# A windowed-attention block on one core: 32-row score tiles in one run, four strips for values and sums, a written-out end

## The chip, the cores and the metric

One core of a Trainium2 chip runs the whole kernel. The metric is the device time of one execution in microseconds; the time before is the median of three executions. The trace and the page come from one further execution, taken with the profiler on.

## The reference

The input x has shape 4 x 96 x 128 x 128. All arithmetic is float32. Two layers are computed, cut here to what matters:

```
y  = layer_norm(x) over the 96 channels, rolled by (-4, -4), cut into windows of 8 x 8 = 64 tokens
q, k, v = y @ qkv_w.T + qkv_b          # 6 heads of 16 channels, q scaled by 1/4
p  = softmax(q @ k.T + mask)           # mask: -100 between parts of a window that wraps round the image
x  = x + (p @ v) @ proj_w.T + proj_b   # rolled back
x  = x + gelu(layer_norm(x) @ w1.T + b1) @ w2.T + b2     # 384 hidden channels
out = x * rsqrt(gamma @ (x * x) + beta)
```

The mask differs from zero in the last column of windows (side by side parts), in the last row of windows (upper and lower parts), and in the corner for both.

## The kernel before, in words

**Tiling.** A unit is one row of 16 windows (8 image rows, 1024 tokens). A half is 8 windows, 512 tokens. There are 64 units and 128 halves (`HALVES`). Within a half, two neighbouring windows form a pair (`PAIRS` = 4), since 2 x 64 tokens fill 128 partitions. Six heads form three head pairs.

**Rounds.** `rounds` (L221) walks over H; in every round each engine runs its list of stages once, each stage for another half: statistics and transposes of half H+4 (`TURN_IN`), normalised rows turned back of H+3 (`TURN_OUT`), q and k of H+1 (`QK`), scores, softmax and v of H (`ATTEND`), products with v of H-1, output projection of H-1 (`PROJECT`), first MLP product of H-2 (`MLP`), second of H-3 (`SETTLE`), the division at the end of H-4 (`DIVIDE`). The order in each list is written by hand in each engine's `steps` (PE L1035, ACT L602, DVE L819, POOL L489, SP L382), and semaphores hold the engines together. Rounds go on with has() guards until the last half has passed all stages.

**PE.** Precise products of 512 tokens go through `in_parts` (L897): three float32r products (high weight by high data, low by high, high by low). POOL's `split_hi`, `split_lo` (L430, L435) make the parts with two instructions over 512 columns each. Scores, v, products with v, and sums of probabilities are plain float32; each such matmul stands as two records in the profile.

**Scores** (`scores` L940). A half is done in two groups of two pairs. q and `k_block` lie in two row tiles of 64 partitions: three heads of 16 channels (48 rows), then eight mask rows, then zeros. `k_block` holds the keys in a block diagonal, so that one matmul of a 64 x 64 tile gives the scores of 3 heads, 64 tokens by 192 columns. A group is 8 matmuls into two PSUM banks. The mask costs no matmul of its own: SP brings mask rows into `y1_hi` each unit (`stage_mask` L322, `place_mask` L331), and the q product, with 105 rows and 128 output columns, passes them on. The two groups use the same two banks, so the second waits for `scores_shifted` of the first.

**Softmax.** For each group DVE takes the row maximum (`max_scores` L777) and subtracts it (`shift_scores` L782), both over 768 columns; ACT exponentiates (`softmax_exp` L556). PE turns the probabilities, three 128 x 128 transposes per pair, into `probs_t_bank` (`turn_probs` L962) and ACT copies 384 columns out (`probs_t_copy` L564), four times a half.

**Values and sums** (`times_v` L971, `sum_probs` L987). Each head pair m writes to its 32 columns of the array (PSUM partitions 32m to 32m+31): 24 matmuls of 64 columns, and three matmuls of 512 columns with a matrix of ones. 96 of the 128 array columns are used. ACT turns the sums into reciprocals with Ln and Exp; DVE multiplies (`divide` L792); POOL splits the product (`split_attended` L450).

**Banks.** Two PSUM banks, `mm_banks`, serve ten products a round in turn (`MM_ITEMS` L245). `mm_wait` (L866) makes a product wait until the one two places earlier has been read out. `turn_banks` serve the layer norms: one bank each takes the turned input and then the rows turned back.

**End of the kernel.** The last halves pass through the same rounds with ever fewer stages in them. A few stages of the last half go elsewhere (`split_last_hidden` L710, `split_last_squares` L722, and `mlp_up` into score banks).

## Time and profile before

| | us |
|---|---|
| median of 3 executions | 1937.88 (1937.69 to 1939.2) |
| the profiled execution's own time | 1939.82 |
| its span, first to last instruction | 1937.9 |
| PE busy | 1878.0 (97%) |
| PE weight loads busy | 1355.8 (70%) |
| DVE busy | 1610.0 (83%) |
| ACT busy | 1638.5 (85%) |
| POOL busy | 1645.4 (85%) |

The clock granted to TensorE is 0.993 of full speed on average. Busy time of an engine is the time in which at least one of its instructions has a record; records of consecutive instructions overlap a little, so the distance from one start to the next is the better price of an instruction in a row. PE's weight loads have rows of their own and run beside its matmuls. DMA engines are busy for 22% of the time.

### The profile page before, as it was taken

Reading aid. Unit: us, or ns where it says so; the run is one execution under the profiler, and the core shown is the slowest. Engines: PE = TensorE matmul, PEld = TensorE weight load, DVE = VectorE, ACT = ScalarE, POOL = GpSimd, SP = SyncE. Lnnn points to the kernel's source line nnn. Section 1 sums busy time; section 2 is a strip of 40 time slices with the busy share of each in tenths; the row PEclk is TensorE's granted clock in tenths of the full one; section 3 lists DMA queues with packets and bytes.
Section 4 is the critical chain, followed back from the end, with each engine's and each line's share of the span. In section 5 each row is a group of like instructions: output and inputs, shape, how many; then the busy total and the mean of one; then the engine's idle time right before and its main releaser. Section 6 shows DMA issues by size and latency. Waiting matters only on the chain.

```text
span 1937.9 us, 70164 instructions
## 1 busy us (share of the span) xinstructions
PE 1878.0 (97%) x26628; PEld 1355.8 (70%) x26628; DVE 1610.0 (83%) x4516; ACT 1638.5 (85%) x2945; POOL 1645.4 (85%) x1801
## 2 busy tenths in 40 slices
PE   5999999999999999999999999999999999999995
PEld 3677777777777777777777777777777777777773
DVE  5888888888888888888888888888888888888873
ACT  2788888888888888888888888888888888888884
POOL 4688888888888888888888888888888888888884
PEclk9999999999999999999999999999999999999997
DMA  3122222122122122122122122122122122122110
GB/s 62 28 42 50 35 51 50 35 51 50 35 51 50 34 52 50 33 53 50 32 54 50 32 53 50 32 53 49 34 53 44 38 52 49 35 51 50 26 31 25
DMA packets 217315, 85.00 MB, mean 44 GB/s; under 512 B 117287, under 2 KB 215913, under 8 KB 216985
## 3 DMA queue, kind: packets, MB, share of 16 engines
q1 hardware_dynamic: 216262, 80.22, 21.4%
q8 instruction: 216, 3.54, 0.8%
q14 instruction: 115, 0.93, 0.2%
q0 software_dynamic: 128, 0.20, 0.1%
q10 hardware_dynamic: 594, 0.12, 0.0%
HBM read 28.03 MB, written 25.17 MB: 27 GB/s over the span
## 4 chain that ended last, share of the span: by engine, by line
PE 95%; DVE 2%; issue 1%; DMA 1%; ACT 1%; SPq 1%; POOL 0%; POOLq 0%; DVEq 0%
PE mm_bank L900 49%; PE score_banks L956 11%; PE probs_t_bank L967 8%; PE pv_bank L981 6%; PE turn_bank L893 6%; PE mm_bank L991 6%; PE mm_bank L934 5%; PE turn_bank L886 4%; SPq L351 0%; DVE y_tok L750 0%; DMA k_block<-k 0%; DVE row_max L779 0%; DMA x_ext<-in_x 0%; DVE shifted L787 0%; DVE x L808 0%
## 5 line engine op out<-in xcount | busy, mean ns | idle before, releaser
L438 POOL TENSOR_TENSOR hidden_lo<-hidden,hidden_hi 128x512 fp32r<-128x512 f32 x382 | 484.6, 1282 | 0.2 <-POOL hidden_hi L433 0.2
L779 DVE TENSOR_REDUCE row_max<-score_banks 128x12 f32<-128x768 f32 x256 | 243.5, 951 | 152.7 <-PE score_banks L956 152.6
L520 ACT ACT_TABLE_LOAD x256 | 328.4, 1283 | 4.5
L750 DVE TENSOR_SCALAR y_tok<-turn_bank,moments,rstd 128x96 f32<-128x96 f32 x1024 | 304.8, 371 | 10.0 <-ACT rstd L531 5.6
L587 ACT ACTIVATE hidden<-mm_bank 128x512 f32<-128x512 f32 x381 | 228.0, 598 | 76.2 <-PE mm_bank L900 60.7
L560 ACT ACTIVATE probs<-shifted 128x768 f32<-128x768 f32 x256 | 216.2, 845 | 65.8 <-DVE shifted L787 65.5
L967 PEld LDWEIGHTS probs_t_bank<-ident_sb,probs 128*128 128x128 f32 x1536 | 200.0, 141 | 82.4 <-issue 2.4
L967 PE MATMUL probs_t_bank<-ident_sb,probs 128*128 128x128 f32 x1536 | 252.2, 272 | 1.4 <-ACT probs_t L566 1.4
L566 ACT ACTIVATE probs_t<-probs_t_bank 128x384 f32<-128x384 f32 x512 | 246.1, 481 | 7.6 <-PE probs_t_bank L967 7.6
L787 DVE TENSOR_TENSOR shifted<-score_banks,row_max 128x768 f32<-128x768 f32 x256 | 245.2, 958 | 8.8
L438 POOL TENSOR_TENSOR y_lo<-y,y_hi 96x512 fp32r<-96x512 f32 x128 | 218.8, 1709 | 23.8 <-POOL y_hi L433 23.3
L433 POOL TENSOR_SCALAR hidden_hi<-hidden 128x512 fp32r<-128x512 f32 x382 | 231.5, 617 | 2.1 <-ACT hidden L587 2.1
L956 PE MATMUL score_banks<-k_block,q 64*64 64x192 f32 x4096 | 227.0, 337 | 4.4 <-DMA k_block<-k 3.7
L956 PEld LDWEIGHTS score_banks<-k_block,q 64*64 64x64 f32 x4096 | 132.6, 133 | 137.6 <-issue 132.9
L739 DVE BATCH_NORM_STATS2 stats<-turn_bank 128x6 f32<-128x96 f32 x1024 | 190.2, 248 | 18.2 <-PE turn_bank L886 17.9
L433 POOL TENSOR_SCALAR attended_hi<-attended 96x512 fp32r<-96x512 f32 x128 | 79.2, 619 | 143.2 <-DVE attended L795 143.2
L438 POOL TENSOR_TENSOR attended_lo<-attended,attended_hi 96x512 fp32r<-96x512 f32 x128 | 165.4, 1293 | 23.8 <-POOL attended_hi L433 23.8
L438 POOL TENSOR_TENSOR x_sq_lo<-x_sq,x_sq_hi 96x512 fp32r<-96x512 f32 x127 | 162.1, 1276 | 23.6 <-POOL x_sq_hi L433 23.6
L900 PE MATMUL mm_bank<-y_hi,w_hi 97*128 97x512 f32 x381 | 171.9, 451 | 0.0
L900 PE MATMUL mm_bank<-hidden_hi,w_hi 128*96 128x512 f32 x384 | 163.0, 425 | 0.8 <-ACT log_den L592 0.7
L900 PE MATMUL mm_bank<-hidden_hi,w_lo 128*96 128x512 f32 x384 | 152.3, 397 | 0.0
L900 PE MATMUL mm_bank<-hidden_lo,w_hi 128*96 128x512 f32 x384 | 152.2, 396 | 0.0
(132 smaller groups left out, 4524.3 us busy)
## 6 DMA issues: line engine op xcount, KB each, us to landing
x_ext<-in_x SPq DMA_DIRECT2D x128, 192.0 KB, 3.3
k_block<-k SPq DMA_DIRECT2D x768, 32.0 KB, 2.1
out<-o_ext SPq DMA_DIRECT2D x128, 192.0 KB, 2.8
mask_stage<-in_qmask SPq DMA_DIRECT2D x64, 32.0 KB
y_hi<-mask_stage SPq DMA_DIRECT2D x64, 32.0 KB
k_block<-in_kmask POOLq DMA_DIRECT2D x2, 96.0 KB, 5.3
w_raw<-in_w_t SPq DMA_DIRECT2D x1, 144.0 KB
w<-in_w_t SPq DMA_DIRECT2D x1, 144.0 KB
```

The lines of the kernel that those rows point to most:

```text
L433: nc.gpsimd.tensor_scalar(hi, whole, 1.0, 1.0, ALU.mult, ALU.mult).then_inc(hi_ready, 1)
L438: nc.gpsimd.tensor_tensor(lo, whole, hi, ALU.subtract).then_inc(is_split, 1)
L520: nc.scalar.preload_act_table_set(name)
L560: nc.scalar.activation(probs[:, g, :, :, :, :].rearrange("t p j r k -> t (p j r k)"), shifted[:, g, :, :, :].rearrange("t i r k -> t (i r ...
L566: nc.scalar.activation(probs_t[:, a % 2, :, p, :], probs_t_bank[:, 0:HEAD_PAIRS * 128] .rearrange("k (p t) -> k p t", p=HEAD_PAIRS), ACT.C ...
L587: nc.scalar.activation(hidden[:, n, :], up_bank(A, a, n), ACT.Gelu).then_inc(gelu_ready, 1)
L750: made = nc.vector.tensor_scalar(y_tok[ln][:, c, :], turn_banks[ln][:, n * DIM:(n + 1) * DIM], moments[ln][:, c, 0:1], rstd[ln][:, c:c + 1 ...
L779: nc.vector.tensor_reduce(row_max[:, g, :, :], group_scores(), op=ALU.max, axis=AX.X)\
L787: nc.vector.tensor_tensor(shifted[:, g, :, :, :].rearrange("t i r k -> t r i k"), group_scores(), row_max[:, g, :, :].unsqueeze(3) .broadc ...
L900: made = nc.tensor.matmul(out, w, x_part, start=first and part == 0, stop=last and part == 2)
L956: made = nc.tensor.matmul(score_banks[64 * n:64 * n + 64, r, p * width:(p + 1) * width], q[rows, unit_slot(a), w * TOKENS:(w + 1) * TOKENS ...
L967: made = nc.tensor.transpose(probs_t_bank[:, m * 128:(m + 1) * 128], probs[:, g, at, m, :, :], ident_sb[:, :])
```

## The change

- Scores: `ROW_TILES` becomes 3. A row tile has 32 rows, which are exactly two heads (q and k in their natural order), so q, wq and y1_hi lose the mask rows and the padding; the q product has 97 rows and 96 output columns. `k_block` has 96 rows. All four pairs of a half are done in one run: 24 matmuls of 32 x 64 tiles and 128 columns, into three banks, one for each row tile (head pair).
- Mask: where a window has one, a further matmul adds it: four rows (`q_quadrants`) by 128 columns (`k_masks`), one for each row tile. That is the last window of each second half, and every window in the last row of windows. The mask DMAs of each unit go; nine small loads at the start take their place.
- Softmax in three groups of 512 columns (one bank each) in place of two of 768. The transposed probabilities go back into the score bank they came from, four transposes for each head pair, and ACT copies 512 columns, three times a half. `probs_t_bank` goes. The run of scores of a half therefore waits for the last copy of the half before (`probs_t_ready`).
- Values and sums on four strips: the fourth strip of 32 array columns takes the last pair of windows of all three head pairs. `times_v` still has 24 matmuls of 64 columns, `sum_probs` six matmuls (three of 384 and three of 128 columns). Ln and Exp of the sums run over 128 x 384. `divide` becomes four DVE instructions: three of 32 x 128 and one of 96 x 384.
- The rounding of the product with v moves from POOL to DVE (`round_attended`). POOL's other splits are taken apart so that an unrelated instruction stands between the two halves of a split.
- All lists and the order of the ten bank users are new. After the round of the last half a list written out by stage (`late`) takes the place of the remaining rounds, for every engine. In it the projection of the last half, the second MLP product and the denominators of the last two halves are plain float32 products without splits, and all Gelu evaluations of the last two halves stand behind one table load.

The core of the diff:

```diff
-ROW_TILES = 2
+ROW_TILES = 3
-GROUPS = 2
-GROUP_PAIRS = PAIRS // GROUPS
+GROUPS = HEAD_PAIRS
+STRIPS = HEAD_PAIRS + 1
+LAST = PAIRS - 1
+MAIN = LAST * 2 * TOKENS
...
         MM_ITEMS = [
-            ("v", ATTEND, v_ready, 1, 1), ("sum", ATTEND - 1, log_sum_made, 1, 1),
-            ("den", DIVIDE, log_den_made, 1, 1), ("k", QK, k_ready, 1, 1),
-            ("mlp2", SETTLE, x3_ready, 1, 1), ("q", QK, q_ready, 1, 1), ("proj", PROJECT, x2_ready, 1, 1),
-            *((f"mlp1_{n}", MLP, gelu_ready, HID_CHUNKS, n + 1) for n in range(HID_CHUNKS)),
+            ("sum", ATTEND - 1, log_sum_made, 1, 1),
+            ("k", QK, k_ready, 1, 1),
+            ("den", DIVIDE, log_den_made, 1, 1),
+            ("q", QK, q_ready, 1, 1),
+            ("mlp2", SETTLE, x3_ready, 1, 1),
+            ("v", ATTEND, v_ready, 1, 1),
+            ("proj", PROJECT, x2_ready, 1, 1),
+            ("mlp1_0", MLP, gelu_ready, HID_CHUNKS, 1),
+            ("mlp1_1", MLP, gelu_ready, HID_CHUNKS, 2),
+            ("mlp1_2", MLP, gelu_ready, HID_CHUNKS, 3),
...
+            def scores(A, a):
+                if has(A - 1):
+                    wait_alone(pe, probs_t_ready, GROUPS * A)
+                wait_alone(pe, q_ready, A + 1)
+                wait_alone(pe, keys_copied[a % 2], 16 * HEADS * (A // 2 + 1))
...
+                for p in range(PAIRS):
+                    cols, w = slice(p * width, (p + 1) * width), (a % 2) * HALF_WINDOWS + 2 * p
+                    for r, n in tiles:
+                        rows = slice(TILE_DIM * r, TILE_DIM * (r + 1))
+                        made = nc.tensor.matmul(score_banks[64 * n:64 * n + 64, r, cols],
+                                                q[rows, unit_slot(a), (w + n) * TOKENS:(w + n + 1) * TOKENS],
+                                                k_block[rows, w + n, :, :],
+                                                start=True, stop=mask_kind(A, w + n) is None)
+                    for r, n in tiles:
+                        kind = mask_kind(A, w + n)
+                        if kind is not None:
+                            rows = slice(TILE_DIM * r, TILE_DIM * r + QUADRANTS)
+                            made = nc.tensor.matmul(score_banks[64 * n:64 * n + 64, r, cols],
+                                                    q_quadrants[rows, :], k_masks[rows, kind, :, :],
+                                                    start=False, stop=True)
...
+                for turn in range(2 * LAST):
+                    at, n = turn // 2, turn % 2
+                    for strip in range(STRIPS):
+                        m, p = (strip, at) if strip < HEAD_PAIRS else (at, LAST)
+                        made = nc.tensor.matmul(pv_bank[32 * strip:32 * strip + 32, first:first + TOKENS],
+                                                v_block[:, (a % 2) * HALF_WINDOWS + 2 * p + n, m, :],
+                                                probs_t[:, a % 2, m, p, n * TOKENS:(n + 1) * TOKENS],
+                                                start=True, stop=True)
...
             def divide(A, a):
+                for m in range(HEAD_PAIRS):
+                    cols = slice(m * 2 * TOKENS, (m + 1) * 2 * TOKENS)
+                    nc.vector.tensor_tensor(attended[32 * m:32 * m + 32, MAIN:HALF], pv_bank[DIM:128, cols],
+                                            inv_sum[DIM:128, cols], ALU.mult)
+                nc.vector.tensor_tensor(attended[0:DIM, 0:MAIN], pv_bank[0:DIM, 0:MAIN],
+                                        inv_sum[0:DIM, :], ALU.mult).then_inc(attended_ready, 1)
+            def round_attended(A, a):
+                dve.wait_ge(attended_ready, A + 1)
+                nc.vector.tensor_copy(attended_hi[0:DIM, :], attended[0:DIM, :]).then_inc(attended_hi_ready, 1)
```

The new lists of a round (SP's is as before without the mask steps):

```
PE:   scores, sum_probs(H-1), times_v(H-1), k, denominators, turn_out(H-2), q, turn_probs 0, second MLP product,
      v, turn_out(H+3), turn_probs 1, project, turn_probs 2, turn_in(H+4), mlp_up 0, mlp_up 1, turn_in(H-1), mlp_up 2
DVE:  max 0, max 1, shift 0, normalise(H-2), shift 1, divide, max 2, round_attended, normalise(H+3), shift 2,
      second residual, split_y2, v_blocks, first residual, outputs, statistics(H+4), statistics(H-1)
ACT:  log table, rstd(H-2), rstd(H+3), log_sums, inverse_sums, k, exp 0, log_den, y(H-2), q, probs_t 0, inv_den,
      exp 1, exp 2, y(H+3), gelu table, probs_t 1, gelu 0, probs_t 2, gelu 1, gelu 2
POOL: split_hidden, wrap_out, rest_of_attended, wrap_x, square, round_y1, round_squares, rest_of_y1, rest_of_squares
```

## Rows read from the trace of the kernel before

**Rows 1.** The page, busy time: engine, busy us (share of span), instructions.

```profile
PE 1878.0 (97%) x26628; PEld 1355.8 (70%) x26628; DVE 1610.0 (83%) x4516; ACT 1638.5 (85%) x2945; POOL 1645.4 (85%) x1801
```

**Rows 2.** PE timeline, one round: start, us, engine, line, operation, out<-in, count.

```profile
961.56 0.88 PE L956 MATMUL score_banks<-k_block,q 64*64 64x192 f32 x16
962.37 0.89 PE L934 MATMUL mm_bank<-wv,y 97*32 97x48 f32 x64
963.08 1.09 PE L981 MATMUL pv_bank<-probs_t,v_block 128*32 128x64 f32 x48
963.97 1.06 PE L991 MATMUL mm_bank<-probs_t,ones_pair_sb 128*32 128x512 f32 x6
964.96 0.88 PE L956 MATMUL score_banks<-k_block,q 64*64 64x192 f32 x16
965.77 0.48 PE L900 MATMUL mm_bank<-x_sq_hi,wgdn_hi 97*96 97x512 f32 x1
...
967.25 0.49 PE L967 MATMUL probs_t_bank<-ident_sb,probs 128*128 128x128 f32 x3
967.57 1.04 PE L893 MATMUL turn_bank<-ident_sb,y_tok 128*96 128x128 f32 x8
...
971.33 0.40 PE L900 MATMUL mm_bank<-y_lo,wq_hi 105*128 105x512 f32 x1
971.75 0.44 PE L900 MATMUL mm_bank<-attended_hi,wproj_hi 97*96 97x512 f32 x1
...
973.10 0.48 PE L900 MATMUL mm_bank<-y_hi,w_hi 97*128 97x512 f32 x1
...
975.65 0.49 PE L967 MATMUL probs_t_bank<-ident_sb,probs 128*128 128x128 f32 x3
976.07 0.88 PE L956 MATMUL score_banks<-k_block,q 64*64 64x192 f32 x16
```

**Rows 3.** DVE timeline of the same round, with idle time before and its releaser.

```profile
962.51 0.96 DVE L779 TENSOR_REDUCE row_max<-score_banks 128x12 f32<-128x768 f32 x1 [1.19 <-PE score_banks L956]
963.50 0.96 DVE L787 TENSOR_TENSOR shifted<-score_banks,row_max 128x768 f32<-128x768 f32 x1
964.38 1.11 DVE L768 COPY v_block<-mm_bank 64x384 f32<-64x384 f32 x2
965.52 2.38 DVE L750 TENSOR_SCALAR y_tok<-turn_bank,moments,rstd 128x96 f32<-128x96 f32 x8
967.81 0.68 DVE L795 TENSOR_TENSOR attended<-pv_bank,inv_sum 96x512 f32<-96x512 f32 x1
968.41 0.94 DVE L779 TENSOR_REDUCE row_max<-score_banks 128x12 f32<-128x768 f32 x1
...
972.69 0.69 DVE L800 TENSOR_TENSOR x<-mm_bank,x_ext 96x512 f32<-96x512 f32 x1 [0.49 <-PE mm_bank L900]
973.36 0.76 DVE L739 BATCH_NORM_STATS2 stats<-turn_bank 128x6 f32<-128x96 f32 x4
```

**Rows 4.** Waits, 200 to 1800 us: us in total, times, longest.

```profile
DVE row_max L779 <- PE score_banks L956: 130.6, 110, 1.2
```

**Rows 5.** Instructions of POOL L438, L433 and DVE L716: duration min/median/max in ns.

```profile
L438 POOL TENSOR_TENSOR y_lo<-y,y_hi x128: 1248/1786/1819, 15.5 to 1846.1; 96x512 fp32r<-96x512 f32 x128
L433 POOL TENSOR_SCALAR x_sq_hi<-x_sq x127: 616/618/2103, 83.7 to 1918.1; 96x512 fp32r<-96x512 f32 x127
L716 DVE CAST hidden_hi<-hidden x2: 413/836/1258, 1917.0 to 1918.1; 128x512 fp32r<-128x512 f32 x2
```

**Rows 6.** The chain that ended last, its end: start, us, what.

```profile
1877.48 0.85 PE score_banks L956 x16
...
1915.70 0.76 DVE x L808
...
1928.21 0.76 DVE x L808
...
1929.71 0.43 DVE x_sq_hi L730
```

More of the change, by code:

```diff
@@ L51 @@
 X_SLOTS = 4
-QKV_CONSTS = 8
-MLP_CONSTS = 14
+QKV_CONSTS = 6
+MLP_CONSTS = 9
 MLP_WEIGHTS = 4
@@ L227, in rounds, with late @@
                 steps(run, H)
+        def late(stage, A, *rest):
+            stage(A, A % (2 * X_SLOTS), *rest)
         def has(at, count=HALVES):
@@ new lines, in window_block, with mm_bank @@
+        MM_ORDER = [(item[0], H + item[1]) for H in range(-TURN_IN - 1, HALVES) for item in MM_ITEMS
+                    if has(H + item[1])] + MM_FINISH
+        MM_PLACE = {item: place for place, item in enumerate(MM_ORDER)}
+        MM_EMPTIED = {item[0]: item[2:] for item in MM_ITEMS}
+        def mm_bank(name, A):
+            return mm_banks[MM_PLACE[name, A] % len(mm_banks)]
+        def mm_bank_emptied(name, A):
+            place = MM_PLACE[name, A] - len(mm_banks)
+            if place < 0:
+                return None
+            other, B = MM_ORDER[place]
+            semaphore, per_half, own = MM_EMPTIED[other]
+            return semaphore, per_half * B + own
@@ L502, in _ @@
             rounds(steps)
+            late(split_hidden, FINAL - 2)
+            late(wrap_out, FINAL - 4)
+            late(square, FINAL - 2)
+            late(round_squares, FINAL - 2)
+            late(rest_of_squares, FINAL - 2)
+            late(wrap_out, FINAL - 2)
+            late(wrap_out, FINAL)
         @block.scalar
@@ L847, in _ @@
             rounds(steps)
+            late(normalise, FINAL - 1, 1)
+            late(divide, FINAL)
+            late(split_y2, FINAL - 1)
+            late(first_residual, FINAL)
+            late(second_residual, FINAL - 2)
+            late(statistics, FINAL, 1)
+            late(outputs, FINAL - 3)
+            late(normalise, FINAL, 1)
+            late(split_y2, FINAL)
+            late(second_residual, FINAL - 1)
+            late(last_squares, FINAL - 1)
+            late(outputs, FINAL - 2)
+            late(second_residual, FINAL)
+            late(last_squares, FINAL)
+            late(outputs, FINAL - 1)
+            late(outputs, FINAL)
         @block.tensor
@@ L1062, in steps @@
                     w1_bias_product()
-                last = H == HALVES - 1 - MLP
-                if not last:
-                    run(mlp_up, MLP, 0)
+                run(mlp_up, MLP, 0)
+                run(mlp_up, MLP, 1)
                 run(turn_in, PROJECT, 1)
-                if not last:
-                    run(mlp_up, MLP, 1)
-                    run(mlp_up, MLP, 2)
-                run(turn_probs, ATTEND, 3)
+                run(mlp_up, MLP, 2)
             rounds(steps)
+            late(times_v, FINAL)
+            late(sum_probs, FINAL)
+            late(turn_out, FINAL - 1, 1)
+            late(denominators, FINAL - 3)
+            last_project()
+            for n in range(HID_CHUNKS):
+                late(mlp_down, FINAL - 2, n)
+            late(mlp_up, FINAL - 1, 0)
+            late(turn_in, FINAL, 1)
+            late(mlp_up, FINAL - 1, 1)
+            late(turn_out, FINAL, 1)
+            late(mlp_up, FINAL - 1, 2)
+            late(denominators, FINAL - 2)
+            for n in range(HID_CHUNKS):
+                late(mlp_up, FINAL, n)
+            last_mlp_down(FINAL - 1)
+            last_mlp_down(FINAL)
+            last_denominators(FINAL - 1)
+            last_denominators(FINAL)
 def kernel(x, L0_conv_norm1_w, L0_conv_norm1_b, L0_conv_qkv_w, L0_conv_qkv_b, L0_conv_proj_w,
```

455 lines of the change are left out of this document (212 added, 243 removed).

## The prediction

> **What bounds the kernel now.** I read the page first [rows 1]: PE is busy for 97% of the span, the other engines for 83 to 85%. A sum over stages would already point to PE, but the share of busy time of pipelined matmuls proves little, so I went to the timeline of one round [rows 2]. There the reader should lay start against start: every PE group begins when the one before it has drained; the only stall inside the round is 0.18 us between the end of the q product (971.33 + 0.24) and the projection (971.75). A round, from one first run of scores to the next, takes 976.07 - 961.56 = 14.51 us. Then the DVE timeline [rows 3]: its list is one dense run with two holes, 1.19 us before the first maximum and 0.49 us before the first residual, both ended by PE. The wait list says that this is so in all rounds [rows 4]: 110 waits in 1600 us, 130.6 us in all. So PE's own work sets the round, DVE has 1.68 us of room, and its occupied time is 14.51 - 1.68 = 12.83 us. The end of the kernel is different [rows 6]: 60.4 us lie between the last half's first scores (1877.48) and the end of the span, and there single engines wait for each other.
>
> **PE's work after, without waits.** What a tiled plain product costs can be read from four groups [rows 2]. Each moves 3072 columns (records x columns). Spread over four tiles, 768 each, they take 0.71 (v, 962.37 to 963.08) and 0.81 us (scores). Over three strips, 1024 each, they take 0.89 (values) and 0.99 (sums). So 256 columns more in every tile cost 0.18 us, and I use that as the price.
> - Scores: 48 records x 128 = 6144 columns in six tiles, 1024 each: 0.81 + 0.18 = 0.99 us, once, in place of twice 0.81. No row has six tiles at once; the bounds are 0.99 and, if only four run at a time, 1536 columns a tile, 1.35 us. I take 0.99, since 2 x 2 tiles already run side by side at the rate of four strips.
> - Values: 0.89 - 0.18 = 0.71. Sums: 0.99 - 0.18 = 0.81. The bounds are these and no gain (0.89, 0.99).
> - Masks: in every second half three matmuls, 256 columns a tile, 0.18 us; in the last of 16 rows of windows 24 matmuls over six tiles, about 0.72 us. On average 0.5 x 15/16 x 0.18 + 0.72/16 = 0.13 us a round.
> - Transposes of probabilities: twelve as before, in three groups for four. v, k, q, denominators, projection and MLP: same columns, so the same slots. Fewer rows and output columns of q change nothing: column count sets these slots.
> - Wait and row moves: DMA of masks goes from SP's queue; it was off the path, worth 0.
>
> Before its first turn_out, PE now does scores 0.99, sums 0.81, values 0.71, k and denominators 1.48 (965.77 to 967.25): 3.99 us. From turn_out to the next scores it took 976.07 - 967.57 = 8.50 us; take off the 0.18 stall, add v 0.71 and three transposes 0.32 (967.25 to 967.57, the fourth group that used to stand earlier): 9.35 us. PE alone: 3.99 + 9.35 + 0.13 = 13.47 us a round, 1.04 less than now.
>
> The Trainium skill ("TensorEngine Tiling (Array Packing)", Tiling Modes) says that 32 x 64 gives eight independent tiles and that changing the mode drains the engine; by its first part the six tiles cost the 0.99 above, and no run here shows it yet.
>
> **DVE's work after** [rows 3]. A subtraction takes 0.88 us start to start for 768 columns (963.50 to 964.38) and the product `attended` 0.60 for 512 (967.81 to 968.41): 0.28 per 256 columns. So each of three maxima and three subtractions costs 0.60, 3.60 in all, against two pairs of 0.99 + 0.88, 3.74: -0.14. `divide`: the large piece 0.60 - 0.14 = 0.46; three pieces of 128 columns between a statistics instruction of 96 columns (0.76 us for four, 0.17 each) and a normalisation of 96 columns (965.52 to 967.81 for eight, 0.29). I take 0.20, near the first, because it has no scalars from memory either: 1.06 in all, +0.46; bounds 0.97 and 1.42. The rounding: 0.43 us in [rows 6], 0.35 start to start. DVE then holds 12.83 - 0.14 + 0.46 + 0.35 = 13.50 us, almost exactly what PE holds. Its 1.68 us of room are gone, and so latency around the round decides.
>
> **What is late next.** I count from the start of a run of scores, masks left out. DVE's first maximum starts 0.95 us after a run of 0.81 (962.51 - 961.56), so at 1.13 after one of 0.99.
> - Loop 1. max, max, shift to 2.93; four normalisations (2.29/2) to 4.08, the last one's tail and signal to 4.23. PE arrives at turn_out of H-2 at 3.99 and waits 0.24. Behind this wait stand q, all later products and the next scores: 4.23 + 9.35 + 0.13 = 13.71 us. It also means that what the values and sums save is mostly waited away: without their 0.36 PE would arrive at 4.35.
> - Loop 2. DVE goes on: shift 0.60, divide 1.06, max 0.60, rounding 0.35, normalise 1.15, shift 0.60, second residual 0.66 (its slot before the 0.49 hole, duration less overlap), split_y2 0.60, v_blocks 1.14 (964.38 to 965.52). The end is at 10.84; with the signal, mlp_up 0, which uses v's bank, may start at 10.94. From there to the next scores PE needs 976.07 - 973.10 less a transposes group, 2.65: 13.59 + 0.13 = 13.72. PE itself would come at 10.93. The two loops tie.
> - The rounding on DVE against POOL [rows 5]. Here two casts in SBUF took 413 and 1258 ns, the second beside a POOL instruction; POOL's rounding took 616 ns as a rule and 2103 once, at that same moment. y_lo took 1248 ns at the start and 1786 in the rounds. Now the rounding stands where POOL is just finishing the split of the hidden values, every round. Bounds: 0 and 0.84 us on loop 2. I take 0.23, since POOL's split should end at about that time.
>
> The Trainium skill ("SBUF — State Buffer", Who interferes with whom) has this as an exclusive lock held for a whole instruction; the trace agrees, with 1258 against 413 ns. By that rule alone the cost would be nothing or the rest of a POOL instruction, never a share.
>
> Other new waits have cover: the next scores wait for the last copy of transposed probabilities, which ACT can do at about 13.0, 0.7 before; the key copies start 2 us earlier in the round than now; POOL gets its last part of the product at 6.8 and has until 9.6. ACT's groups change by -0.2 us. If these covers were gone each would cost its overlap, 0.1 to 0.7.
>
> A round: 13.72 + 0.23 = 13.95 us, 0.56 less. Some 124 of the 128 rounds are full: 69.4 us.
>
> **The end** [rows 6]. Between the second residuals of the last two halves lie 12.5 us, in which POOL splits squares for one and DVE hidden values for the other. In the new list three plain products lie there; one moves 1024 columns, at most 0.99 us, say 2.6 for three: 9.9 us less. The cast of the last square and its rest, about 1.1, go. With the other splits I take 13; bounds 5 and 20. The start I leave at 0.
>
> Sum: 69.4 + 13 = 82.4. Against the profiled execution: span 1937.9 to 1855.5, its own time 1939.82 to 1857.4. The median shown is 1.94 below the latter, so the forecast is 1855.5.
>
> **Rivals.**
> - PE bound (0.15). The normalisation and v_blocks are never late; for it: 0.24 us is a small miss and orders can absorb it. Then 13.47 a round, 129 + 13 = 142: 1796. Against: both loops miss it by the same amount.
> - Six tiles do not run together (0.18). For it: no row shows more than four. Scores 1.35, and since both loops begin with them the round is 14.31: 25 + 13 = 38, 1900.
> - DVE lock, on the other side (0.20). The rounding is blocked each round for the 0.84 of [rows 5], 0.61 more than I took, and the divide pieces cost 0.32 each, 0.36 more; v_blocks comes 0.97 later, mlp_up 0 waits, and the round is 14.92. That is +51 - 13 = +38: 1976. It decides from 0.66 us above what I took (0.56, plus 13/124); the lock alone gives 14.56, 1931. Against: DVE could only be blocked so long if POOL started a long instruction just before, every time.
> - The forecast, two tied loops at 13.75 to 14.15 (0.47): 1830 to 1880.
>
> A difference of 0.2%, 3.9 us, is about what a measurement of this kernel can tell. Faster: 0.47 + 0.15 + 0.15 + 0.04 = 0.81; slower 0.15; same 0.04. The range 1795 to 1935 holds all but half of the lock's case and the outer part of the PE case.
>
> **What would show it.** Scores in 0.99 us and values in 0.71: the price by tile is right. A wait of turn_out for the normalisation of about 0.2 us, or of mlp_up 0 for v_blocks, in each round: the loops. The rounding at 0.42 with few at 1.2: the lock is small. DVE idle before its first maximum below 0.5 us. I am wrong if scores take over 1.3 us, if PE waits for something on ACT or POOL, or if PE has no wait at all.

## The result, and the profile after

| | before | changed |
|---|---|---|
| median | 1938.54 us (1937.69 to 1940.3, 4 runs) | 1890.55 us (1888.51 to 1891.02, 4 runs) |
| profiled execution's own time | 1939.82 | 1888.51 |
| its span | 1937.9 | 1886.6 |
| round, start of scores to next, median | 14.51 | 14.07 (first halves of a unit), 14.25 (second halves) |
| last scores to the end of the span | 60.4 | 55.4 |

The changed kernel takes 0.9749 of the time before (95% interval 0.9732 to 0.9766), 48 us less. The forecast was 1855.5: the direction is right, the size was to be 82 us. The time lies inside the wide range on record (1795 to 1935) but outside the band of the forecast's own case (1830 to 1880), and nearer to the rival in which six tiles don't run together (1900) than to the forecast. All the accounting below is between the two profiled spans: 51.3 us less, where 82.4 were forecast, so 31.1 us are to be explained.

The page, busy time by engine, the row that answers to [rows 1]:

```profile
PE 1829.9 (97%) x30179; PEld 1376.4 (73%) x30179; DVE 1729.0 (92%) x5278; ACT 1586.8 (84%) x2950; POOL 1538.1 (82%) x1661
```

DVE went from 83% to 92%. PE still shows 97%, as before, and this says little: the holes that matter in a round are of 0.05 to 0.2 us and lie inside the modelled tails of its records. They are read from starts. This is the PE timeline of one round of a first half (no masks) in the middle of the kernel, to be laid beside [rows 2]; columns are start, us, engine, line, operation, out<-in, count.

```profile
936.81 1.12 PE L996 MATMUL score_banks<-k_block,q 32*64 32x128 f32 x48
937.86 0.52 PE L1037 MATMUL mm_bank<-probs_t,ones_pair_sb 128*32 128x384 f32 x3
...
938.53 0.86 PE L1027 MATMUL pv_bank<-probs_t,v_block 128*32 128x64 f32 x48
939.32 0.47 PE L935 MATMUL mm_bank<-y_hi,wk_hi 97*96 97x512 f32 x1
...
939.87 0.39 PE L935 MATMUL mm_bank<-y_lo,wk_hi 97*96 97x512 f32 x1
940.31 0.44 PE L935 MATMUL mm_bank<-x_sq_hi,wgdn_hi 97*96 97x512 f32 x1
...
940.82 0.40 PE L935 MATMUL mm_bank<-x_sq_lo,wgdn_hi 97*96 97x512 f32 x1
941.10 0.64 PE L928 MATMUL turn_bank<-ident_sb,y_tok 128*96 128x128 f32 x4
...
947.83 0.50 PE L921 MATMUL turn_bank<-ident_sb,x_ext 96*128 96x96 f32 x4
948.26 0.47 PE L935 MATMUL mm_bank<-y_hi,w_hi 97*128 97x512 f32 x1
...
950.88 1.12 PE L996 MATMUL score_banks<-k_block,q 32*64 32x128 f32 x48
```

Start against start: scores hold 1.05 us, sums 0.67, values 0.79. Three short stalls can be seen. The denominators begin 0.44 after the last matmul of k, where 0.23 is the step between matmuls of this kind: 0.21 us. Then turn_out begins 0.28 after the last matmul of the denominators: 0.05. And mlp_up 0 begins 0.43 after turn_in, where the next turn_in of the same round (949.73 to 950.01) needs 0.28: 0.15. Without the three the round would be 13.66. The first of them ends soon after ACT has taken the logarithm of the sums out of the bank that the denominators need (ACT's timeline, done at 940.16):

```profile
939.69 0.47 ACT L586 ACTIVATE log_sum<-mm_bank 128x384 f32<-128x384 f32 x1
```

The DVE timeline of the same round, beside [rows 3]:

```profile
938.01 1.29 DVE L791 TENSOR_REDUCE row_max<-score_banks 128x8 f32<-128x512 f32 x2 [0.55 <-PE score_banks L996]
...
939.82 1.23 DVE L762 TENSOR_SCALAR y_tok<-turn_bank,moments,rstd 128x96 f32<-128x96 f32 x4
940.96 0.68 DVE L799 TENSOR_TENSOR shifted<-score_banks,row_max 128x512 f32<-128x512 f32 x1
941.67 0.91 DVE L809 TENSOR_TENSOR attended<-pv_bank,inv_sum 32x128 f32<-32x128 f32 x3
942.59 0.55 DVE L811 TENSOR_TENSOR attended<-pv_bank,inv_sum 96x384 f32<-96x384 f32 x1
943.07 0.68 DVE L791 TENSOR_REDUCE row_max<-score_banks 128x8 f32<-128x512 f32 x1
943.66 0.41 DVE L817 CAST attended_hi<-attended 96x512 fp32r<-96x512 f32 x1
...
947.00 1.11 DVE L780 COPY v_block<-mm_bank 64x384 f32<-64x384 f32 x2
```

The list is dense from the first maximum on; v_blocks is over at 948.11 and mlp_up 0 starts on PE at 948.26. The hole ahead of the first residual [rows 3] is gone. The waits of 200 to 1800 us, first DVE's and then those of PE's weight loads, beside [rows 4]; columns are who waited, for whom, us in total, times, longest:

```profile
DVE row_max L791 <- PE score_banks L1004: 31.5, 57, 1.5
DVE row_max L791 <- PE score_banks L996: 15.3, 50, 0.6
...
PEld turn_bank L928 <- DVE y_tok L762: 45.2, 105, 0.6
```

DVE's waits for scores fell from 130.6 us to 46.8. The third row is the wait that the forecast named: the weight loads of turn_out wait for the normalised rows in nearly every round, 0.43 us each. A load waits earlier than its matmul would have to start: in the round above only 0.05 us reaches PE's own starts.

Durations beside [rows 5] (min/median/max in ns, first and last start):

```profile
L817 DVE CAST attended_hi<-attended x127: 412/413/417, 49.0 to 1838.9; 96x512 fp32r<-96x512 f32 x127
L809 DVE TENSOR_TENSOR attended<-pv_bank,inv_sum x384: 292/293/298, 47.0 to 1853.1; 32x128 f32<-32x128 f32 x192
```

The chain at the end, beside [rows 6]. Table loads on ACT stand at the start of its last 41 us:

```profile
1845.66 1.28 ACT L542
...
1877.74 0.76 DVE x L829
```

### The profile page after: what moved, and what is told of

It is laid out like the page before. It is cut to its first block, busy times and chain, and to the rows that moved or that the text cites. A ratio compares the mean times of both kernels' runs of the same rounds, so it can differ in the third digit from the quotient of the medians.

```text
span 1886.6 us, 77050 instructions
## 1 busy us (share of the span) xinstructions
PE 1829.9 (97%) x30179; PEld 1376.4 (73%) x30179; DVE 1729.0 (92%) x5278; ACT 1586.8 (84%) x2950; POOL 1538.1 (82%) x1661
## 4 chain that ended last, share of the span: by engine, by line
PE 89%; DVE 6%; issue 3%; ACT 1%; DMA 0%; SPq 0%; POOL 0%; DVEq 0%; POOLq 0%
PE mm_bank L935 45%; PE score_banks L1013 9%; PE turn_bank L928 8%; PE score_banks L996 7%; PE mm_bank L969 5%; PE turn_bank L921 4%; DVE y_tok L762 4%; PE pv_bank L1027 4%; PE mm_bank L1040 3%; PE mm_bank L1037 2%; PE score_banks L1004 1%; SPq L368 0%; DVE shifted L799 0%; PE mm_bank L1087 0%; DMA k_block<-k 0%
## 5 line engine op out<-in xcount | busy, mean ns | idle before, releaser
L574 ACT ACTIVATE probs<-shifted 128x512 f32<-128x512 f32 x384 | 241.0, 628 | 148.3 <-DVE shifted L799 146.6
L791 DVE TENSOR_REDUCE row_max<-score_banks 128x8 f32<-128x512 f32 x384 | 251.5, 683 | 59.6 <-PE score_banks L1004 39.4
L799 DVE TENSOR_TENSOR shifted<-score_banks,row_max 128x512 f32<-128x512 f32 x384 | 260.4, 678 | 0.0
L463 POOL TENSOR_TENSOR x_sq<-x 96x512 f32<-96x512 f32 x126 | 130.7, 1037 | 138.5 <-DVE x L829 138.5
L1013 PE MATMUL score_banks<-ident_sb,probs 128*128 128x128 f32 x1536 | 231.2, 273 | 0.6 <-ACT probs L574 0.5
L580 ACT ACTIVATE probs_t<-score_banks 128x512 f32<-128x512 f32 x384 | 227.7, 593 | 2.2 <-PE score_banks L1013 0.7
L1013 PEld LDWEIGHTS score_banks<-ident_sb,probs 128*128 128x128 f32 x1536 | 187.7, 141 | 43.1 <-ACT probs L574 2.2
L928 PE MATMUL turn_bank<-ident_sb,y_tok 128*96 128x128 f32 x1024 | 165.3, 284 | 23.4 <-DVE y_tok L762 19.8
L996 PE MATMUL score_banks<-k_block,q 32*64 32x128 f32 x6144 | 148.6, 275 | 4.1 <-DMA k_block<-k 3.8
L996 PEld LDWEIGHTS score_banks<-k_block,q 32*64 32x64 f32 x6144 | 114.5, 132 | 50.7 <-issue 50.7
```

The lines of the kernel that those rows point to most:

```text
L574: nc.scalar.activation(probs[:, g, :, :, :].rearrange("t p j k -> t (p j k)"), shifted[:, g, :, :].rearrange("t i k -> t (i k)"), ACT.Exp)\
L791: nc.vector.tensor_reduce(row_max[:, g, :], group_scores(g), op=ALU.max, axis=AX.X)\
L799: nc.vector.tensor_tensor(shifted[:, g, :, :], group_scores(g), row_max[:, g, :].unsqueeze(2) .broadcast_to([128, PAIRS * TILE_HEADS, TOKE ...
L928: made = nc.tensor.transpose(turn_banks[ln][0:DIM, n * 128:(n + 1) * 128], y_tok[ln][:, c, :], ident_sb[:, :])
L996: made = nc.tensor.matmul(score_banks[64 * n:64 * n + 64, r, cols], q[rows, unit_slot(a), (w + n) * TOKENS:(w + n + 1) * TOKENS], k_block[ ...
L1013: made = nc.tensor.transpose(score_banks[:, g, p * 128:(p + 1) * 128], probs[:, g, p, :, :], ident_sb[:, :])
```

## The experiments

All are edits of the changed kernel, and all ratios are to the kernel before, run on the same chip. "Round" is the median distance of two starts of scores, first halves of a unit / second halves (those with a mask). "Mean" is that of all rounds between the scores of halves 4 and 123, "end" the time from the last half's first scores to the end of the span; these three columns are of the profiled execution.

| version | us (range) | ratio, 95% | round | mean | end |
|---|---|---|---|---|---|
| before | 1938.54 | 1 | 14.51 / 14.51 | 14.588 | 60.4 |
| changed | 1890.55 (1888.51 to 1891.02) | 0.9749, 0.9732 to 0.9766 | 14.07 / 14.25 | 14.222 | 55.4 |
| changed, again | 1889.75 (1888.43 to 1892.53) | 0.9743, 0.9727 to 0.9759 | 14.07 / 14.25 | 14.228 | 55.3 |
| tables | 1885.21 (1883.78 to 1886.1) | 0.9715, 0.9701 to 0.973 | 14.07 / 14.24 | 14.222 | 50.6 |
| vfirst | 1898.05 (1895.48 to 1899.14) | 0.978, 0.9765 to 0.9795 | 14.13 / 14.31 | 14.281 | 54.2 |
| strips3 | 1875.25 (1872.66 to 1876.46) | 0.9663, 0.9648 to 0.9677 | 13.94 / 14.16 | 14.127 | 55.4 |
| poolround | 1868.49 (1867.03 to 1869.18) | 0.9633, 0.9619 to 0.9647 | 13.92 / 14.05 | 14.061 | 55.0 |
| nomask | 1873.92 (1870.56 to 1876.1) | 0.9661, 0.9646 to 0.9676 | 14.07 / 14.07 | 14.117 | 54.3 |
| qfirst | 1900.86 (1898.76 to 1903.36) | 0.9797, 0.9781 to 0.9813 | 14.08 / 14.25 | 14.317 | 55.5 |
| best | 1876.12 (1875.42 to 1880.32) | 0.9678, 0.9663 to 0.9692 | 13.99 / 14.03 | 14.153 | 49.3 |
| loop1 | 1864.18 (1863.2 to 1865.23) | 0.9612, 0.9598 to 0.9626 | 13.87 / 14.05 | 14.073 | 48.1 |
| best2 | 1861.48 (1857.9 to 1862.51) | 0.9595, 0.9579 to 0.9612 | 13.81 / 14.03 | 14.013 | 50.0 |
| best3 | 1854.53 (1853.73 to 1855.2) | 0.9564, 0.9551 to 0.9577 | 13.81 / 14.03 | 13.976 | 49.8 |
| rows2 | 1883.69 (one run) | | 14.03 / 14.23 | 14.179 | 56.4 |

**The changed kernel once more** (after_again), no edit.

> The changed kernel as it is, as the yardstick for the experiments beside it. Every theory expects about 1890 us, rounds of 14.06 us (even halves) and 14.25 us (odd halves, with masks).

It came out the same within 1 us, so differences of some 4 us between these versions can be told.

**Where the round is held: the rounding back on POOL** (poolround).

```diff
# DVE's list
-                run(round_attended, PROJECT)
# POOL
             def rest_of_attended(A, a):
+                split_hi(attended_hi[0:DIM, :], attended[0:DIM, :], attended_ready, attended_hi_ready, A + 1)
```

> The rounding of the product with v goes back from DVE to POOL; all else as changed. DVE has 0.34 us less in a round before the v blocks and the low part of y2, POOL 0.62 more. Theory (DVE's list up to y2_lo and the v blocks is 0.15 us late for mlp_up 0, the rest of its length is hidden): the wait before mlp_up 0 goes, 13.92 us for even halves, 18 us less in all; not the full 0.34. Rival (the length of DVE's list sets the round as such): 13.73, 42 us less. Other rival (POOL now delivers the split product late for the projection): the same 14.07 or more.

The round fell to 13.92 in first halves and by 0.20 to 14.05 in second ones, and the kernel by 22 us (medians), where 18 were expected. PE's timeline of a first half shows at turn_in and mlp_up 0 which stall went:

```profile
938.19 0.50 PE L921 MATMUL turn_bank<-ident_sb,x_ext 96*128 96x96 f32 x4
938.47 0.48 PE L935 MATMUL mm_bank<-y_hi,w_hi 97*128 97x512 f32 x1
```

mlp_up 0 follows turn_in by 0.28, without a hole, and the stall ahead of the denominators stands as before (last matmul of k 930.23, first of theirs 930.67: 0.21). So of a first half's round in the changed kernel 0.15 us are due to DVE's list up to v_blocks: with 0.34 us less in that list the round gave back no more. What holds it next is the subject of loop1 below. That the rounding costs DVE only its own 0.34 us start to start, and no block by POOL, is seen in its row above (412 to 417 ns, 127 times).

**The fourth strip undone** (strips3): values and sums on 96 columns and three strips again, reciprocals over 96 x 512, one division. The cut shows the division alone.

```diff
-                for m in range(HEAD_PAIRS):
-                    cols = slice(m * 2 * TOKENS, (m + 1) * 2 * TOKENS)
-                    nc.vector.tensor_tensor(attended[32 * m:32 * m + 32, MAIN:HALF], pv_bank[DIM:128, cols],
-                                            inv_sum[DIM:128, cols], ALU.mult)
-                nc.vector.tensor_tensor(attended[0:DIM, 0:MAIN], pv_bank[0:DIM, 0:MAIN],
-                                        inv_sum[0:DIM, :], ALU.mult).then_inc(attended_ready, 1)
+                nc.vector.tensor_tensor(attended[0:DIM, :], pv_bank[0:DIM, :],
+                                        inv_sum[:, :], ALU.mult).then_inc(attended_ready, 1)
```

> Only the four strips are undone: values and sums on three strips of 32 columns again, reciprocals over 96 x 512, and the division is one instruction. Scores, order and end stay. PE then has 0.10 (values 0.89 for 0.79) and 0.32 us (sums 0.99 for 0.67) more in a round, DVE 0.80 less (0.60 for 1.40). Theory (both loops bind, the saving on PE is waited away at turn_out and the division on DVE costs what the strips bring): a round changes by less than 0.15 us, 14.0 to 14.2 for even halves. Rival (PE's work alone sets the round): 0.4 us more, 14.48, 54 us in all. Other rival (DVE's list alone sets it): 0.8 less as far as PE lets it, 13.7 or below.

Taking this part back made the kernel 14.5 us faster. The two timelines of one round, PE's and DVE's (its lines stand four lower than in the changed kernel from there on; this is a second half, with a mask):

```profile
943.43 1.06 PE L1033 MATMUL mm_bank<-probs_t,ones_pair_sb 128*32 128x512 f32 x6
944.31 1.07 PE L1023 MATMUL pv_bank<-probs_t,v_block 128*32 128x64 f32 x48
...
945.85 0.39 PE L931 MATMUL mm_bank<-y_lo,wk_hi 97*96 97x512 f32 x1
946.08 0.39 PE L931 MATMUL mm_bank<-x_sq_hi,wgdn_hi 97*96 97x512 f32 x1
```

```profile
946.49 0.68 DVE L799 TENSOR_TENSOR shifted<-score_banks,row_max 128x512 f32<-128x512 f32 x1
947.09 0.68 DVE L807 TENSOR_TENSOR attended<-pv_bank,inv_sum 96x512 f32<-96x512 f32 x1
947.68 0.68 DVE L791 TENSOR_REDUCE row_max<-score_banks 128x8 f32<-128x512 f32 x1
```

On PE sums hold 0.88 and values 1.00, 0.42 us more than on four strips; but the denominators now follow k at once and no stall is left in the round. On DVE shift, division and maximum stand 0.60 and 0.59 apart, where the changed kernel needs 0.71 and 1.40: 0.92 us less. So the fourth strip gives PE 0.42 us. In the changed kernel PE waits 0.41 of it away again, and three further groups hold 0.14 more there than here (denominators 0.74 for 0.69, turn_out 0.40 for 0.36, v 0.87 for 0.82): together the 0.13 by which the changed kernel's round is longer. DVE pays 0.92 us for it, and it had no room. Both rivals on record, that the round would be longer by PE's work or as short as 13.7 by DVE's, fell. The expected bound of 0.15 us held as well, but the range of 14.0 to 14.2 did not: at 13.94 the round is shorter, so DVE's pieces cost more than the strips bring.

**v_blocks ahead of split_y2 on DVE** (vfirst).

```diff
-                run(split_y2, MLP)
                 run(v_blocks, ATTEND)
+                run(split_y2, MLP)
```

> DVE copies v into its blocks before it makes the low part of y2, 0.6 us earlier in the round. Theory (DVE's list to the v blocks holds up the first MLP product through the bank of v): the wait of 0.15 us before mlp_up 0 goes, a round takes 13.91 and 14.10 us, 18 to 20 us less in all. Rival (PE's own slots set the round; the gap before mlp_up 0 is a change of tiling, not a wait): no change, within 3 us.

A miss: expected was a gain of 18 to 20 us with rounds of 13.91, measured a loss of 8.3 against the run beside it with rounds of 14.13. The timelines show why.

```profile
952.63 1.11 DVE L780 COPY v_block<-mm_bank 64x384 f32<-64x384 f32 x2
953.78 0.69 DVE L771 TENSOR_TENSOR y_lo<-turn_bank,y_hi 96x512 fp32r<-96x512 f32 x1
```

```profile
954.52 0.50 PE L935 MATMUL mm_bank<-y_hi,w_hi 97*128 97x512 f32 x1
```

The first fence is DVE's, the second PE's. mlp_up 0 multiplies y2, and so waits for its split as well as for v's bank; whichever of the two DVE does last holds it (954.47 against 954.52). The first theory had put the whole wait down to the bank. What sets the round is DVE's list up to the end of both, and in this order it ends no earlier: 11.42 us after the start of the scores (943.05), for 11.30 before.

**Do six score tiles run side by side?** (rows2)

```diff
-                tiles = [(r, n) for r in range(ROW_TILES) for n in range(2)]
+                tiles = [(r, n) for r in range(ROW_TILES if A == 0 else 2) for n in range(2)]
```

> The scores of the third row tile (third head pair) are left out in all halves but the first, so its bank holds older numbers and the output is not the reference's. 32 records in four tiles in place of 48 in six, 1024 columns in each tile either way. Theory (six tiles run side by side, the time is that of one tile's columns): the run of scores takes 0.99 to 1.05 us, as now. Rival (PE works through records at a rate, whatever their tiles): 0.70 us.

```profile
961.84 1.10 PE L996 MATMUL score_banks<-k_block,q 32*64 32x128 f32 x32
962.87 0.52 PE L1037 MATMUL mm_bank<-probs_t,ones_pair_sb 128*32 128x384 f32 x3
```

Four tiles with 32 records hold 1.03 us, six with 48 hold 1.05. The third row tile costs 0.02 us, so six tiles run side by side as four do; if they did not, the run of scores would have needed the prediction's 1.35. The Trainium skill ("TensorEngine Tiling (Array Packing)", Tiling Modes) lists this mode as eight independent tiles, and the pair of runs agrees for six of them.

**The price of the masks** (nomask).

```diff
-                    for r, n in tiles:
+                    for r, n in ():
                         kind = mask_kind(A, w + n)
# and the matmul of the scores stops its group itself
```

> The changed kernel without its mask matmuls (the mask is left out of the scores, so the output is not the reference's). Theory: odd halves fall from 14.25 to 14.07 and the halves of the last row of windows from 14.95 to 14.07; 56 x 0.18 + 8 x 0.88 + 8 x 0.70 = 23 us less. Rival (masks run in the shadow of the other waits): less than 10 us.

The second halves fell from 14.25 to 14.07 and the whole kernel by 16.6 us. The number on record, 23, was a slip of arithmetic: 60 rounds with one masked window, 0.18 each, and seven rounds of the last rows of windows, 0.88 each (14.95 for 14.07), make 17. The prediction's 0.13 a round, 16.6 us, holds for the medians; between the profiled executions the difference is 12.4 us, in part because the start took 2.8 us longer in this one.

**q ahead of turn_out** (qfirst), on PE and ACT, so that the wait for the normalised rows has something in front of it.

```diff
# PE's list
-                run(turn_out, MLP, 1)
                 run(project_q, QK)
+                run(turn_out, MLP, 1)
# ACT's list: log_sums ahead of rstd(H+3), q_copy ahead of y_copy(H-2)
```

> The two other waits of PE are taken out by order alone, four strips and DVE's list untouched: the sums' Ln stands one step earlier on ScalarE (denominators waited 0.21 us for its bank), and the q product stands before turn_out of the half two back (with q's copy before y's on ScalarE). Theory (mlp_up 0 waits for DVE anyway): PE comes to mlp_up 0 some 0.25 us earlier and waits that much longer, round unchanged at 14.07 within 0.05. Rival (loop 1, normalise to turn_out, binds): 13.8, 30 us less.

The round stayed at 14.08, as expected where DVE's list holds it. But the kernel became 10 us slower (medians), by something else. Waits of PE, 80 to 1830 us, of this kernel:

```profile
PE mm_bank L935 <- ACT k L567: 13.2, 51, 0.5
PE pv_bank L1027 <- issue: 10.7, 14, 1.3
```

The first row costs nothing in a round that DVE holds anyway. The "issue" row and others like it are idle stretches of about 1 us for which the profile names no releaser. Counted as the rounds of halves 4 to 122 that are longer than the median of their kind by 0.5 us or more, they take 9.6 us in the kernel before (11 rounds), 1.6 us in the changed one (2 rounds) and 11.9 us here (13 rounds). (Another 3 us of this execution's loss lie ahead of half 4.) One of the changed kernel, behind the products with v (they start at 966.84 and hold 0.79):

```profile
968.86 0.45 PE L935 MATMUL mm_bank<-y_hi,wk_hi 97*96 97x512 f32 x1 [1.16 <-issue]
```

The traces say more about them. DMA queue 8 carries packets of kind "instruction", 16 KB each; this is its row on the page of the changed kernel (packets, MB, share of the DMA engines):

```profile
q8 instruction: 241, 3.95, 0.9%
```

PE has 30179 matmul records there, 125 for each packet. Taken one by one against the median step at the same place of a round (rounds of the last rows of windows left out), PE's starts show four stretches of over 0.3 us in the changed kernel and 14 in qfirst. From one to the next it is always a whole number of steps of 124.8 records, to within 0.02 of a step, and in all 18 a packet of this queue had landed 1.2 to 1.7 us before PE went on, which is so at only 6 to 8% of all its starts. In the kernel before, 13 rounds are 2704 records, which is 22 packets of 123, and its 11 long rounds stand in two series, each 13 rounds apart. So I read the stretches as PE waiting for the next block of its own program at places where it runs through many small matmuls; this is inferred from the traces, and no run varied it.

**One table load ahead of the end** (tables).

```diff
             rounds(steps)
+            late(load_tables, FINAL - 1, "natural_log_exp_and_others")
             late(rstd_of, FINAL - 1, 1)
```

> One table load (Ln and Exp in one set) ahead of the written-out end of ScalarE's list. Theory: the end gained only 4.9 of the 13 us that were forecast because every Ln and every Exp there brings a table load of its own (1.28 us each, at least three of them between the last sums and the product with their reciprocal); with the one load, 4 to 7 us less in all, rounds unchanged at 14.06 and 14.25. Rival: the loads lie beside waits for PE, which runs there at a lower clock, and less than 1.5 us is gained.

ACT's timeline at the start of the written-out list, first of the changed kernel, then with the load:

```profile
1845.66 1.28 ACT L542 ACT_TABLE_LOAD   x1
...
1848.79 1.28 ACT L586 ACT_TABLE_LOAD   x1
```

```profile
1845.84 1.28 ACT L534 ACT_TABLE_LOAD   x1
...
1847.58 0.47 ACT L586 ACTIVATE log_sum<-mm_bank 128x384 f32<-128x384 f32 x1
```

In the changed kernel each of the eight Ln and Exp ahead of the last Gelus has a load of its own, 1.28 us; with the set that holds both functions loaded ahead there is one for all. The end shrank by 4.8 us, the kernel by 4.5 (against the run beside it), as expected.

**Putting the pieces together** (best, loop1, best2, best3). All have the rounding on POOL and the table load. best adds qfirst's orders.

> Both of these together and the one table load at the end. Theory of two tied loops: with all three waits gone PE's own slots are left, 14.07 - 0.15 - 0.21 - 0.05 = 13.66 us for even halves; 50 us from the rounds and 4.5 from the end, about 1835 us. Rival (a further loop just below, over ACT or POOL): 13.8 to 13.95, 1850 to 1870.

Round 13.99, not the 13.66 of the theory: a further wait, as in the rival on record, is there. The time of 1876 us is above the rival's 1850 to 1870 too; 13 of this version's rounds hold the idle stretches above, 12 us in all. Timelines of PE and ACT (lines one higher than in the changed kernel):

```profile
1025.15 0.40 PE L936 MATMUL mm_bank<-x_sq_lo,wgdn_hi 97*96 97x512 f32 x1
1025.80 0.44 PE L936 MATMUL mm_bank<-y_hi,wq_hi 97*96 97x512 f32 x1 [0.25 <-ACT k L568]
```

```profile
1025.08 0.58 ACT L568 ACTIVATE k<-mm_bank 96x512 f32<-96x512 f32 x1
```

q uses the bank of k, and the copy of k stands behind the reciprocals on ACT: 0.42 us late. loop1 therefore keeps PE's order and puts ACT's in the order log_sums, rstd(H+3), k_copy, inverse_sums, so that the bank of the sums, which the denominators need, is read earlier.

> Rounding on POOL, one table load at the end, and on ScalarE the sums' Ln and k's copy moved ahead, so that neither the denominators nor q wait for a bank; PE's order as changed, turn_out of the half two back before q. Theory (loop 1: scores, two maxima, a subtraction, four normalisations, then turn_out): turn_out cannot start before 4.29 us of the round whatever comes before it, so the 0.21 us won at the denominators is waited again there, and an even half stays at 13.92 us; about 1864 us. Rival (waits of PE add up one by one): 13.7, 1840 us.

13.87 and 1864.18 us, close to the 13.92 and 1864 expected; the rival of 13.7 fell. The denominators now follow k at once (0.23), but turn_out starts 0.55 us after their last matmul (932.08 to 932.63), for 0.28 in the changed kernel: what was won at the one wait is waited again at the other, for the normalised rows. best2 takes PE's order of qfirst with it.

> The same with the q product before turn_out. In the kernel before this one q waited 0.42 us for its bank, because k's copy stood behind the reciprocals on ScalarE; that is mended. Theory: no wait of PE is left, 13.6 to 13.7 us for even halves and 13.85 for odd ones; 1835 to 1845 us, unless the idle stretches of about 1 us that PE has in some rounds with no releaser (11 in the kernel before this one) come again, which give 1850. Rival (another loop): 13.9 as in the kernel with turn_out first.

13.81 and 1861 us, where 13.6 to 13.7 and at most 1850 us were expected: a miss. q still waits 0.24 us for the copy of k (1015.84 to 1016.08, the copy ends at 1015.94). best3 moves k's product ahead of the products with v, and its copy right behind log_sums:

```diff
# PE's list
-                run(times_v, ATTEND - 1)
                 run(project_k, QK)
+                run(times_v, ATTEND - 1)
# ACT's list
+                run(k_copy, QK)
                 run(rstd_of, TURN_OUT, 0)
-                run(k_copy, QK)
                 run(inverse_sums, PROJECT)
```

> As the kernel before it (rounding on POOL, q before turn_out, one table load), with the k product ahead of the products with v, and k's copy right behind the sums' Ln on ScalarE. There q still waited 0.24 us for its bank (13.81 us an even half). Theory: that wait goes and PE's slots alone are left, 13.56 us for even halves, 13.74 to 13.80 for odd ones, where DVE is close; 1835 to 1840 us. Rival (DVE's list, 13.2 us long without the rounding, with the signal between them makes a loop of its own): 13.75 or more, 1855 to 1860.

```profile
1007.95 0.47 PE L936 MATMUL mm_bank<-y_hi,wk_hi 97*96 97x512 f32 x1
...
1008.48 0.39 PE L936 MATMUL mm_bank<-y_lo,wk_hi 97*96 97x512 f32 x1
1008.80 0.88 PE L1028 MATMUL pv_bank<-probs_t,v_block 128*32 128x64 f32 x48
```

No wait is left at q, but the round is still 13.81. k now parts two groups of tiles: the values start 0.32 after its last matmul, where 0.23 is the step, and k itself some 0.1 late behind the sums. That is what the removed wait had been worth. The 13.56 us and 1835 to 1840 us expected were missed. The number of the rival on record came out (13.75 or more), but not its mechanism, as PE waits for nothing of DVE's in this round. It is the fastest version, 1854.53 us, 0.9564 of the time before (0.9551 to 0.9577); against best2 the round is no shorter, and the gain of 7 us comes for the larger part from the long rounds: none in best3, five with 6.5 us in best2, 3.1 of them in one. Three strips together with these orders was not run.

## Why the prediction was right in direction and too large

**What held.** One masked window 0.18 (0.18 measured; a half of the last row 0.88 for 0.72); scores 1.05 for 0.99; values and sums together 1.46 for 1.52. Taken singly, values took 0.79 for 0.71 and sums 0.67 for 0.81, since the order of the two is new: on three strips, too, whichever stands first is the shorter (values before sums 0.89 and 0.99, sums before values in strips3 0.88 and 1.00). By place the prices were right to 0.04. The rival of tiles that don't run together is refuted by the scores' 1.05 and by rows2. Two loops with DVE in them do hold the round, and both waits that the forecast named are there, at mlp_up 0 with 0.15 us and at turn_out with 0.05 for 0.24. The rival of PE alone fell: PE waits 0.41 us in a round. The rival on DVE's lock fell in its first half, while the price of a division piece in its second, 0.32, was nearly right (0.31). One sign of being wrong that was on record did appear: PE waits for ACT, 0.21 us a round.

**The round: 14.07 in place of 13.59, masks and lock left out.** Taken along the forecast's second loop:
- The maximum starts 1.20 after the scores for 1.13: +0.07.
- The step that failed most is the price of the division, "I take 0.20, near the first": each piece of 32 x 128 is 0.31 from the next (293 ns in its row). The row of the normalisation, 0.29, was much the nearer one. (The upper bound of 1.42 reckons 0.32 a piece; with 0.29 it would be 1.33, and the prediction doesn't say where the rest is from.) 1.40 for 1.06: +0.34. The step into the first piece is 0.71 where 0.60 is usual: +0.11, gone in strips3 with the pieces.
- The rest of DVE's list, and the signal: -0.01. PE from mlp_up 0 on: 2.62 for 2.65, -0.03.
- The sum is +0.48. The first loop was off as well: PE's work from turn_out to the next scores is 9.63 without its stall (forecast 9.35), as v holds 0.87 instead of 0.71, and turn_out stands in two groups. Ahead of turn_out the forecast had overlooked a wait: the denominators use the bank of the sums, whose logarithm ACT ends at 940.16, 0.21 us too late. "Other new waits have cover" was wrong there. As loop1 shows, this wait costs next to nothing by itself: without it turn_out waits instead.

**The lock.** I took 0.23 for the rounding and it was 0: the 127 casts took 412 to 417 ns. POOL at the cast of the round above (it starts at 943.66):

```profile
942.87 0.20 POOL L492 COPY o_ext<-o_ext 96x32 f32<-96x32 f32 x1
944.26 1.28 POOL L447 TENSOR_TENSOR attended_lo<-attended,attended_hi 96x512 fp32r<-96x512 f32 x1 [1.18 <-DVE attended_hi L817]
```

POOL has ended its split of the hidden values and a short copy, and waits for the cast. It was idle beside all 127 casts, since the phase is the same in every round; my term was a mean of two cases that don't mix. The Trainium skill ("SBUF — State Buffer", Who interferes with whom) gives an exclusive lock held for a whole instruction, so nothing or a rest and never a share. The rows fit that, but with POOL idle beside every cast they don't test it. The term also made the forecast look better than its steps were: the round without masks and lock was 0.48 too short, and 0.23 for something that cost nothing covered nearly half of it. That is luck.

**From round to kernel.** Forecast: 13.95 against 14.51, 0.56 in 124 rounds. Measured means: 14.222 against 14.588, 0.366. The mean before is 0.08 above the one round that I had read, since 11 of its rounds held an idle stretch of about 1 us; the changed kernel has 8 us less of them, a gain that no step of the forecast contains. Without it the miss of the rounds would be larger. The rounds of halves 4 to 122 give 43.5 us, the first ones 3.5, and the four before the last scores lose 0.7: 46.3 for 69.4.

**The end: 5.0 us for 13.** This is the lower bound on record. The step on the last two second residuals held: they lie 2.75 us apart (1874.99 and 1877.74), 9.8 less than in [rows 6], forecast 9.9. From the last residual to the end it is 8.9 for 9.7. What failed is what stands ahead of them, which the forecast left at nothing: from the last scores to the first of the two residuals it took 38.2 us and takes 43.8. Table loads are 4.7 of these 5.6 us: in tables the stretch is 39.2. The rest was not taken apart, but the stretches by granted clock say where to look (columns: window, length, PE, PEld, DVE, ACT and POOL busy with counts, granted clock, DMA share, GB/s):

```profile
1853.90:1855.00 1.10, 1.03 (x2) 0.46 (x3) 0.62 (x2) 1.07 (x3) 0.00 (x0) 0.50 0.00 0
...
1864.80:1872.00 7.20, 7.11 (x19) 5.26 (x20) 0.72 (x2) 3.53 (x7) 0.00 (x0) 0.55 0.00 0
```

After PE's two waits of 3.6 and 2.5 us behind the loads, and again after one of 3.7 us, the granted clock is at the lower of its two levels, 1.2 GHz, and a matmul of 512 columns takes 0.43 us start to start instead of 0.23. The kernel before shows the same at its end (0.52 of full speed from 1905 to 1915). So in both kernels a wait in the end cost more than its length.

## What to carry to other kernels

Before work is moved to an engine with room, count what room is left once the first engine has become faster: here PE's gain of 0.42 us a round was bought with 0.92 us of DVE, and the version without it was 14.5 us faster. A small instruction can cost more than its share of a large one (128 columns 0.31 us, 512 columns 0.60); price pieces by the row of an instruction of the same shape, or by the upper bound. When a bank or a split is named as what a product waits for, list everything else that it waits for before moving one of them, and when the end is written out by hand, put the table load there by hand too.

## What the runs showed of the hardware

- A DVE product of 32 x 128 from PSUM takes 293 ns and 0.31 us start to start; one of 96 x 384 takes 554 ns, of 96 x 512 677.
- The price of a tiled plain product goes by the columns of one tile: 1024 columns of scores took 1.03 us on four tiles and 1.05 on six. Place counts too: three strips of 1024 columns took 0.88 as the first and 1.00 as the second group of a pair. In best3 the untiled product between two tiled groups began about 0.1 us late, and so did the group behind it.
- Without a set loaded ahead, Ln and Exp in turn cost a load of 1.28 us each in the written-out end; in the rounds, where the set is loaded ahead, one load serves them all.
- Idle stretches of PE of about 1 us without a releaser made 2 rounds of the changed kernel long and 13 of qfirst, which differs from it only in the order of the lists, and alone moved the time by 10 us. They stand at the borders of the 16 KB packets of the queue that carries instructions. A version should not be judged by one round when differences are this small.
